# Cross-attention tiles in pairs, and four smaller moves in a four-layer cross-attention kernel

## What is computed

```python
def _L0(...):                       # mixed experts by token type
    x += self_attention(rms(x))     # 16 heads of 16, causal
    x += cross_attention(rms(x) @ cq_w, ctx @ ckv_w) @ cdense_w   # 16 heads of 8, 1500 keys, no mask
    x += silu(mi @ gate) * (mi @ up) @ down
def _L1(...):                       # fusion
    mem = ctx @ W_mem.T
    mc = softmax(x @ mem.T / 16) @ mem
    gate = sigmoid([x, mc] @ W_gate.T + b_gate)
    return rms(x + gate * mc)
def _L2(...), _L3(...):             # twice the same with other weights
    q = layernorm(x) @ Wq           # 16 heads of 64, masked keys
    x += tanh(attn_gate) * (softmax(q k^T / 8) v @ Wo)
    x += tanh(ff_gate) * (gelu(layernorm(x) @ W1) @ W2)
```

## Time and profile before

| | before |
|---|---|
| median of three runs (lowest, highest) | 1476.83 us (1475.7, 1477.4) |
| the profiled execution's own time; its span | 1476.38 us; 1474.6 us |
| PE busy, of the span | 1403.8 us, 95% |
| VectorE (DVE), ScalarE (ACT), GpSimd (POOL) busy | 61%, 39%, 38% |
| chain that ended last: PE, DVE, POOL | 84%, 8%, 3% |
| mean granted clock of PE | 0.993 of 2.4 GHz |

### The profile page before, as it was taken

One profiled execution on the slowest core, in us unless ns is written; L12 is line 12 of the kernel. 1 busy time (PEld: TensorE's weight loads), 2 busy tenths in 40 slices (PEclk: granted clock), 3 DMA queues, 4 the chain that ended last, 5 costly groups with the idle time before them and its releaser, 6 DMA issues.

```text
span 1474.6 us, 20618 instructions
## 1 busy us (share of the span) xinstructions
PE 1403.8 (95%) x7850; PEld 740.6 (50%) x7851; DVE 906.7 (61%) x1429; ACT 581.3 (39%) x880; POOL 553.7 (38%) x385
## 2 busy tenths in 40 slices
PE   6979899999999989998998999999999999999998
PEld 3446555555555544444654455555344355555344
DVE  6896766666667616421226788887433778888540
ACT  1264366666666652001442344444122434444121
POOL 2630388888888891000001144452000144453000
PEclk9999999999999999999999999999999999999999
DMA  7000623232323204004842011110042001110000
GB/s 274 0 2 20 165 70 90 67 92 71 88 66 92 52 13 191 0 0 174 335 124 71 0 39 39 40 39 1 0 122 70 1 27 39 39 39 13 1 0 25
DMA packets 45019, 95.62 MB, mean 65 GB/s; under 512 B 6860, under 2 KB 28892, under 8 KB 44908
## 3 DMA queue, kind: packets, MB, share of 16 engines
q1 hardware_dynamic: 44912, 94.21, 21.0%
HBM read 72.04 MB, written 0.97 MB: 50 GB/s over the span
## 4 chain that ended last, share of the span: by engine, by line
PE 84%; DVE 8%; POOL 3%; issue 2%; ACT 2%; DMA 0%; SPq 0%; DVEq 0%; ACTq 0%; POOLq 0%
PE psum L1658 23%; PE psum L2175 10%; PE psum L1899 5%; PE psum L1875 5%; PE psum L1849 4%; PE psum L2107 4%; PE psum L1832 3%; PE psum L2138 3%; PE psum L1818 3%; POOL XN L708 3%; PE psum L2165 2%; PE psum L2170 2%; DVE WA L1341 2%; PE psum L2167 2%; PE psum L2166 2%
## 5 line engine op out<-in xcount | busy, mean ns | idle before, releaser
L1341 DVE TENSOR_REDUCE WA<-psum 112x2 f32<-112x1000 f32 x192 | 229.8, 1200 | 89.9 <-PE psum L1849 89.9
L708 POOL TENSOR_TENSOR XN<-XN,WBZ 125x896 f32<-125x896 f32 x128 | 266.5, 2082 | 16.8 <-POOL XN L708 0.9
L1052 ACT ACTIVATE WA<-psum,y_bias 125x448 f32<-125x448 f32 x192 | 118.6, 633 | 208.9 <-PE psum L2170 190.4
L933 ACT ACTIVATE WBZ<-psum 125x896 f32<-125x896 f32 x192 | 175.5, 915 | 43.9 <-PE psum L1875 33.3
L2175 PE MATMUL psum<-WA,ctxN 125*128 125x448 f32 x384 | 180.9, 554 | 0.8 <-ACT WA L1052 0.7
L740 POOL TENSOR_TENSOR XN<-const,y_max 112x896 bf16<-112x896 f32 x32 | 75.2, 2350 | 246.2 <-DVE y_max L1557 189.2
L731 POOL TENSOR_SCALAR ctxT<-ctxT 128x375 f32<-128x375 f32 x32 | 56.2, 1756 | 250.9 <-ACT std L806 248.4
L1557 DVE CUSTOM_DVE_ANT_0 XA<-psum,WA 112x375 bf16<-112x375 f32 x240 | 125.3, 541 | 37.6 <-PE psum L2138 36.6
L1875 PE MATMUL psum<-R 100*125 100x224 f16 x768 | 110.7, 266 | 0.0
L1570 DVE RECIPROCAL WBZ<-WBZ 128x224 f32<-128x224 f32 x68 | 105.1, 1546 | 0.1
L1875 PEld LDWEIGHTS psum<-R 100*125 100x125 f16 x768 | 78.9, 136 | 28.3 <-issue 25.0
(11 more groups left out here) (255 smaller groups left out, 2337.9 us busy)
## 6 DMA issues: line engine op xcount, KB each, us to landing
R<-WA SPq DMA_DIRECT2D x192, 93.8 KB, 2.2
WA<-in_ctxT SPq DMA_DIRECT2D x14, 750.0 KB, 4.3
ctxT<-in_ctxT SPq DMA_DIRECT2D x11, 750.0 KB, 4.2
ctxN<-in_ctx SPq DMA_DIRECT2D x32, 192.0 KB, 2.5
ctxT<-in_ctxT SPq DMA_DIRECT2D x32, 187.5 KB, 2.4
R<-in_ctx SPq DMA_DIRECT2D x7, 768.0 KB, 7.3
R<-in_ctxT SPq DMA_DIRECT2D x7, 750.0 KB, 7.2
WA<-in_ctx SPq DMA_DIRECT2D x6, 768.0 KB, 6.4
```

The lines of the kernel that those rows point to most:

```text
L708: nc.gpsimd.tensor_tensor(z_sum[b % 2][0:TK, :], first[0:TK, :], z_p[t % 4][0:TK, :], ALU.add)\
L933: nc.scalar.activation(z_p[t % 4][0:TK, :].rearrange("p (k n) -> p k n", k=2), psum[0:TK, s:s + 2, 0:2 * GC], ACT.Exp, scale=float(CHD0) * ...
L1052: nc.scalar.activation(y_pT[t][0:TK, g * HALF:(g + 1) * HALF], bank[2 + u % 3][0:TK, 0:HALF], ACT.Exp, bias=y_bias[0:TK, bass.ds(b * NT + ...
L1341: V.tensor_reduce(z_mx[0:PR, r:r + 3:2, c], psum[0:PR, lo:lo + 2, 0:PC], AX_X, ALU.max)\
```

## The change

- Cross-attention goes in steps of two tiles: on PE the scores of tiles t+2 and t+3, one unit, `attended` of t, on step 8 the turning of the maxima, `attended` of t+1, in the last step all three sums, and then half a piece, a unit, half a piece (on step 8 the unit ahead of both halves). ScalarE does two exponentials, then the evacuations; `evacuate` comes in the batch's own last step. VectorE takes both maxima before `low_keys` and `invert`. The pieces are made on steps 0, 2, 4 (values) and 6, 8, 10 (keys).
- POOL's `divide` moves behind its first addition, `quotient` behind its fourth.
- The second `q1` product (evacuated from bank 6) moves behind `m_scored(0)`.
- VectorE reads its branch word and branches before the gated products; the reciprocals of `n4` are cut in two, and centring of `nq` half 0 stands between the halves of the second.
- `projected` goes in pairs on PE, with four slots of `XA` (the other half's are used too).

```diff
 exps(0, 0)                                        # ScalarE
+exps(0, 1)
 for b in range(B):
-    for t in range(NT):
...
+    for t in range(0, NT, 2):
+        for u in (t + 2, t + 3):
+            if u < NT:
+                exps(b, u)
+            elif b + 1 < B:
+                exps(b + 1, u - NT)
+            if b + 1 < B and t == TURN_AT and u == t + 2:
+                shifts(b + 1)
+        if t + 2 == NT:
+            evacuate(b)
+        if b + 1 < B and t in VALUES_AT:
+            values(b + 1, VALUES_AT[t])
+        if b + 2 < B and t in KEYS_AT:
+            high_keys(b + 2, KEYS_AT[t])
```

```diff
 for b in range(B):                                # POOL
-    if b > 0:
-        divide(b - 1)
     for t in range(1, SUMS + 1):
+        if b > 0 and t == 2:
+            divide(b - 1)
...
-        if b > 0 and t == 3:
+        if b > 0 and t == 4:
             quotient(b - 1)
```

```diff
-    for t in range(NT):                           # VectorE
-        for m, k in ahead(b, t):
+    for t in range(0, NT, 2):
+        for m, k in ahead(b, t) + ahead(b, t + 1):
             maximum(m, k)
             if k == UNITS - 1:
                 combine(m)
+        if b + 2 < B and t in KEYS_AT:
+            low_keys(b + 2, KEYS_AT[t])
-        if b > 0 and t == 3:
+        if b > 0 and t == 2:
             invert(b - 1)
```

```diff
+    for t in range(0, NT, 2):                     # PE
+        units = ahead(b, t) + ahead(b, t + 1)
+        for u in (t + 2, t + 3):
...
+            scores(b, u)
+        for m, k in units[0:1]:
+            unit(m, k)
+        attended(b, t)
+        if b + 1 < B and t == TURN_AT:
+            turn_maxima(b + 1)
...
+        for m, k in units[1:-1]:
+            unit(m, k)
+        attended(b, t + 1)
...
+        if t + 2 == NT:
+            for x in range(ADDED):
+                sums(b, x)
+        if t == TURN_AT:
+            for m, k in units[1:][-1:]:
+                unit(m, k)
+        for side in range(2):
+            if b + 1 < B and t in VALUES_AT:
+                values(b + 1, VALUES_AT[t], side)
+            if b + 2 < B and t in KEYS_AT:
+                keys(b + 2, KEYS_AT[t], side)
+            if side == 0 and t != TURN_AT:
+                for m, k in units[1:][-1:]:
+                    unit(m, k)
```

```diff
 m_scored(0)                                       # PE, fusion
+fusion_queries(1)
+emptied(pe, ("q1", 1))
```

```diff
 def gated(walk):                                  # VectorE, behind the branch
+    for h in range(2):
+        for m in range(KD):
+            emptied(dve, ("mgate", h, m))
...
+    V.memset(y_sum, 1.0).then_inc(sem("x2_first_sum"), 1)
     for h in range(2):
         dve.wait_ge(sem("n4_std"), h + 1)
-        normalised(h)
+        normalised(h, 0)
         if h == 1:
             centre("nq", 0, 0)
+        normalised(h, 1)
         fused_scale(h)
```

```diff
-    for m in range(XT + 1):                       # PE, projected
-        if m < XT:
+    for g in range(XT // 2 + 1):
+        for m in range(2 * g, min(2 * g + 2, XT)):
...
+        for k in range(max(2 * g - 2, 0), 2 * g):
             emptied(pe, ("av", l, h, k))
```

More of the change, by code:

```diff
@@ L170, in schedule @@
     for h in range(2):
-        ev.add(("q1", h), "act")
+        ev.add(("q1", h), "act", h and 6)
     for h in range(2):
@@ L1511, in fed_forward, with normalised @@
                 emptied(dve, ("ff2", l, h, KD - 1))
-            def normalised(h):
-                then(V.reciprocal(std[:, half(h)], std[:, half(h)]))
+            def normalised(h, part):
+                at = slice(h * HT + part * HT // 2, h * HT + (part + 1) * HT // 2)
+                then(V.reciprocal(std[:, at], std[:, at]))
             def fused_scale(h):
@@ L1941, in _ @@
             warm(6, 4)
+            scores(0, 1)
             for b in range(B):
-                for t in range(NT):
-                    for m, k in ahead(b, t)[0:1]:
+                for t in range(0, NT, 2):
+                    units = ahead(b, t) + ahead(b, t + 1)
+                    for u in (t + 2, t + 3):
+                        if u < NT:
+                            scores(b, u)
+                        elif b + 1 < B:
+                            if b + 1 == EARLY and u == NT:
+                                pe.wait_ge(sem("z_queries1"), STACKED)
+                            scores(b + 1, u - NT)
+                    for m, k in units[0:1]:
@@ L1945, in _ @@
                         unit(m, k)
+                    attended(b, t)
                     if b + 1 < B and t == TURN_AT:
                         turn_maxima(b + 1)
-                    for turn in range(2):
-                        if b + 1 < B and t in VALUES_AT and VALUES_AT[t][1] != turn:
-                            values(b + 1, *VALUES_AT[t])
-                        if b + 2 < B and t in KEYS_AT and KEYS_AT[t][1] != turn:
-                            keys(b + 2, *KEYS_AT[t])
-                        if turn == 0 and t + 1 < NT:
-                            scores(b, t + 1)
-                        elif turn == 0 and b + 1 < B:
-                            if b + 1 == EARLY:
-                                pe.wait_ge(sem("z_queries1"), STACKED)
-                            scores(b + 1, 0)
-                        if turn == 0:
-                            for m, k in ahead(b, t)[1:2]:
-                                unit(m, k)
@@ L1962, in _ @@
-                    attended(b, t)
                     if b == B - 1 and t >= COOL:
                         warm(7, 1)
-                sums(b, 0)
-                if b + 2 < B:
-                    keys(b + 2, *KEYS_AT[NT])
-                for i in range(1, ADDED):
-                    sums(b, i)
+                    for m, k in units[1:-1]:
+                        unit(m, k)
+                    attended(b, t + 1)
+                    if b == B - 1 and t + 1 >= COOL:
+                        warm(7, 1)
```

59 lines of the change are left out of this document (19 added, 40 removed).

## The result

The changed kernel takes **1461.36 us** (median of four runs, 1454.48 to 1464.87) against 1477.12 of the kernel before on the same chip: a ratio of 0.9889, 95% interval 0.9847 to 0.9931. The forecast was 1453.9, range 1447.5 to 1462.5. The runs go with TensorE's mean granted clock: 1454.48 had 0.992, 1458.28 had 0.991, 1464.43 and 1464.87 had 0.984. The profiled execution is one of the long ones.

What follows compares the result with a forecast made beforehand. TensorE (PE) was taken to bound the cross-attention, busy 313.8 of 318 us. Savings 16.0 - 0.3 + 3.5 + 3.7 = 22.9 from 1476.38 gave 1453.5; with 0.45 for the median, 1453.9 us, range 1447.5 to 1462.5.

Steps and rivals of the forecast that it cites:

- Part 1: Cross-attention in pairs of tiles: batch period 23.44 us against 24.51, 16.0 us saved over the stage with its ends.
- rival D: Cross-attention: unit to attended at its upper bound, 0.1 more on each of 78 steps, 7.8 us, total 1461.7; chance 0.10.
- Rival A: Cross-attention: only cuts count, regular steps gain nothing; batch 23.74, 3.9 us saved over 13 batches, total 1457.8; chance 0.18.
- turn step: Cross-attention step that turns the maxima: 3.80 us plus 0.34 of waits for VectorE and the copy, 4.14.
- rival B: Cross-attention: POOL paces at 23.15 us, PE needing only 23.10 without waits; 17.7 us saved, total 1450.1; chance 0.12.
- the 1.2 that I had set as the limit: Sign in cross-attention: POOL would wait no more than 1.2 us between batches.
- rival C: Cross-attention: VectorE paces, units 2.2 us apart instead of 1.71, 24.7 us lost, total 1492.5; chance 0.05.
- The turn's place: Cross-attention: turned maxima between two attended tiles leave and enter no cut, costing 0.38 us there.
- Part 2: Fusion queries: first scores move ahead, but the exponential's table load makes the first exponential 0.3 us later.
- Part 3: Norm: VectorE's earlier branch, split reciprocals and earlier centring, variance in 1.77 us; 3.5 us saved, bounds 2.0 and 5.0.
- upper bound of 5.0: Norm: up to 5.0 us saved if the clock's fall is also spared where PE next idles, before the queries.
- Part 4: Layers' gated projections in pairs: fewer cuts save 4.9 us, variance waits 0.6 twice; 3.7 saved, bounds 2.5 and 4.9.

Runs made afterwards that it cites:

- a_last: Changed kernel plus six spare matmuls only before the third unit of batch 0's first step, its longest wait: 1453.48 us, ratio 0.9863 to the kernel before.
- a0_after: The changed kernel run again, unchanged, for the spread of its runs: 1463.04 us over six runs, ratio 0.9922 to the kernel before.
- a1_fill: Changed kernel plus seven spare matmuls in the three waits of batch 0's first step: 1454.55 us, ratio 0.9872 to the kernel before.

## Why the prediction was right, and where it was not

**Part 1, steps of a pair: right.** Value step 3.63 forecast, 3.62 measured where no unit waits; keys 3.60 against 3.59; last step 4.81 against 4.73. Unit to attended was 0.35, as forecast: rival D, which put 0.45 there, falls, and the price of a unit hangs on the unit, not on what follows. Rival A, that only changes of cut count and a regular step stays at 3.71, falls with it: its batch was 23.74 long, the measured one is 23.60, and the two steps in which no unit waits are the 3.62 and the 3.59. The distances that the forecast had to assume came out too: from two scores to the unit 0.86 (0.39 and 0.48), from two attended tiles to the values 0.89 (392.99 to 393.88; 0.40 and 0.49), from the values to the unit 0.63. The period came out 0.16 long: the first units of two value steps and of the turn step come 0.06 to 0.07 late, and the turn step took 4.29 against 4.14. I had those units as safe by 0.03 to 0.16. That VectorE makes them late is not shown: the maximum that they wait for ends 0.15 before them, and other units follow theirs by 0.05 to 0.09. In the turn step the second unit comes 1.81 behind the first (forecast 1.92), and the keys behind it wait 0.20 for ScalarE's copy, where 0.04 was charged. 13 times 0.16 is the 2.1 in the bill.

**POOL: right on the place, wrong on the size.** In the steady batches POOL does not pace (rival B falls), but it waits 1.59 between batches, above the 1.2 that I had set as the limit. That limit did not follow from my own sums, which give 23.44 less 22.09, 1.35. The divides are 23.60 apart, TensorE's period. POOL's own loop, 23.15 by the forecast, is seen in the first batches of a_last: 23.07 to 23.09, with waits of 1.11 to 1.17. VectorE does not pace either (rival C falls).

**The turn's place: near in the total, what it is worth was not borne out.** That the turn between attended tiles "leaves and enters nothing" brought no gain that can be measured: a kernel with the turn in its old place has the same step of 4.29. The pairs make the gain, not the turn.

**What failed: the clock in batch 0.** The forecast took the granted clock of the stage as it stood (1.00 from 192 to 510), and priced batch 0 by its load of queries alone. It used, a unit of batch 0 that waits 0.77 for VectorE, only as a distance. Read beside the new order of the instructions, the same row would have said that the change takes the values from between the units there and so lengthens waits that already existed. That term was missing: 10.6 us in the profiled run, 4.9 in the shorter one of a0_after. It is shown from both sides: spare matmuls in the wait bring the changed kernel to 1453.5 to 1454.6, where the forecast has 1453.9, and longer waits in the kernel before cost it 17.4 us by the medians (five runs of six), 13 of them spared when TensorE is kept busy with the same lateness. That the median stayed within the range is owed to width, not to foresight.

**Part 2: right.** 0.3 later forecast, 0.34 measured, for the reason given (the load behind the second copy). The stretch at 1.2 GHz in the scores behind it (1.7) was not foreseen.

**Part 3: right, with the clock counted once where it comes twice.** Branch 1.2 of 1.2, centring 0.8 of 0.8, variance 1.77; 3.4 of 3.5. The forecast's upper bound of 5.0, the stretch in front of the queries spared as well, is what after shows (5.1 from the fusion to the layers). That was luck of the run: the same kernel's other profile (a0_after) has a stretch of 3.4 us there, from 778.8, and shows 3.4 (103.40 against 106.82).

**Part 4: right.** 1.8 in each layer, 3.6 of 3.7, the variance's wait 0.57 against 0.6. Another 1.3 came from a stretch at 1.2 GHz of before that is missing.

## What to carry to other kernels

A reordering that gives TensorE longer runs of one kind takes the fillers out of the places where it waits for another engine; go through those places at the head of a stage and at its tail, not only the steady batch, and fill the longest wait with matmuls whose result nobody reads. A saving that sits behind a load of a table, or any fixed cost that used to be hidden, needs that cost moved as well: split and early load pay only together. And when parts of a change are tested singly, compare them from mark to mark in the trace, because short stretches at 1.2 GHz come and go with any shift in time and are as large as the parts themselves.

## What the runs showed of the hardware

With TensorE busy without a gap (in the longest, for 40.61 of 41.00 us) the granted clock stayed at 1.2 GHz for 13.7, 27.3 and 41.0 us in three profiles, and for different lengths in different runs of one program. By the Trainium skill (TensorE: Matmul & The Clock Gate, What's actually happening) an engine that keeps busy is given the full clock again. In the norm and the fusion that came after 3.4 us, and here the trace agrees. In the tail of the cross-attention it took 6.8 us (after, 6.67 of them busy) and 10.2 us (a1_fill, 9.81 busy), in batch 0 up to 41.0, and there the measurement decides. Why it lasts so long there is open. The load of the DMA engines alone is not it: in front of the fall they were busy for 0.95 to 1.01 of the time, but for 0.97 in a1_fill and 0.98 in a_last as well, over the same piece of the program.

The waits in front of the fall (0.51 to 1.39 us) are shorter than some that did no harm (3.64 before the fusion's scores in a_last). The kernel before waits 0.77, 0.24, 0.28 and 0.78 at this place, and none of its 39 runs in the three series has a clock below 0.993; with 0.51, 0.82 and 0.77 it fell to 0.978 in five runs of six. Which of these waits counts, and how the time between them does, was not separated.
